# Tokens of a vision tower: one product of 128 rows per tile, coarse levels folded through the fusing matrix, table gathers issued without holds

## What is computed

```python
def _level(x, idx, W, b, p, gp):
    Bsz, C, H, _ = x.shape
    h = H // p
    t = x.reshape(Bsz, C, h, p, h, p).transpose(0, 2, 4, 3, 5, 1).reshape(Bsz, h * h, p * p * C)
    t = t[:, idx]
    t = t.reshape(Bsz, h * h // gp, gp * p * p * C)
    return t @ W.T + b
...
outs = [_level(x, idx, W, b, p, GP) for idx, W, b, p in Ws]
n_tokens = outs[0].shape[1]
outs = [outs[0]] + [_interp_linear(o, n_tokens) for o in outs[1:]]
y = jnp.concatenate(outs, axis=-1)
return y @ Wf.T + bf
```

## Time and profile before

| | |
|---|---|
| median of 3 runs | 1001.75 us (1001.4 to 1006.43) |
| profiled execution, first to last instruction | 1014.8 us |
| profiled execution, own time | not listed apart from its span |
| busy: TensorE, VectorE, ScalarE, GpSimd | 743.6, 697.2, 672.0, 345.9 us |
| mean granted TensorE clock | 0.796 |

### The profile page before, as it was taken

How to read it: one execution, slowest core, us unless ns; L and a number is a source line. 1 busy time by engine, 2 the same in 40 slices (tenths; PEclk the granted TensorE clock), 3 DMA queues, 4 the chain that set the end, 5 groups by cost and what they waited for, 6 DMA issues and landing times. The chain is left out here.

```text
span 1014.8 us, 19178 instructions
## 1 busy us (share of the span) xinstructions
PE 743.6 (73%) x7062; PEld 537.8 (53%) x7063; DVE 697.2 (69%) x1403; ACT 672.0 (66%) x1229; POOL 345.9 (34%) x260
## 2 busy tenths in 40 slices
PE   2987373344299547999997488867775898999985
PEld 1464141122277324589996444324444467899974
DVE  4159998999599888745443475986998875444542
ACT  1267956999799657755554369578983661676663
POOL 6620460000000000357776424580001202477763
PEclk9979555555599768999999879555556798999999
DMA  5224485000121318623333456380003942233332
GB/s 168 71 90 130 138 234 169 1 23 1 47 75 69 122 45 289 200 54 59 57 56 47 90 233 254 117 297 35 2 2 105 344 169 71 37 54 58 59 45 32
DMA packets 61883, 105.26 MB, mean 104 GB/s; under 512 B 9678, under 2 KB 43618, under 8 KB 61554
## 3 DMA queue, kind: packets, MB, share of 16 engines
q1 hardware_dynamic: 45426, 87.77, 25.6%
q0 software_dynamic: 16384, 16.53, 10.4%
HBM read 76.39 MB, written 27.87 MB: 103 GB/s over the span
## 5 line engine op out<-in xcount | busy, mean ns | idle before, releaser
L2301 DVE COPY m_xgT<-m_px 128x768 f16<-128x768 f16 (+1 forms) x46 | 22.9, 497 | 123.5 <-PE m_px L2146 123.5
L2268 ACT ACTIVATE m_pu<-m_pu,m_b,m_unit 128x256 f32<-128x256 f32 (+1 forms) x138 | 63.5, 509 | 60.9 <-PE m_pu L2178 58.4
L2309 DVE SCALAR_TENSOR_TENSOR m_hT<-m_pu,m_unit,m_hT 128x512 f16<-128x512 f32 (+1 forms) x138 | 86.4, 663 | 17.4 <-ACT m_hT L2261 17.2
L1084 ACT ACTIVATE a_ex<-m_pieces,a_nb 128x256 bf16<-128x256 f16 x192 | 94.6, 560 | 5.4 <-DVE a_nb L1110 5.4
L922 PE MATMUL a_pp<-a_room 16*128 16x256 bf16 x240 | 56.1, 412 | 39.8 <-DVE m_pieces L1098 31.9
L2272 ACT ACTIVATE m_pu<-m_pu,m_unit 128x512 f32<-128x512 f32 (+1 forms) x69 | 41.1, 597 | 62.7 <-PE m_pu L2178 61.7
L2261 ACT ACTIVATE m_hT<-m_pu,m_unit 128x512 f16<-128x512 f32 (+1 forms) x138 | 81.6, 636 | 0.0
L2112 POOL DMA_INDIRECT m_xg<-xn_d,m_token x70 | 70.0, 1000 | 32.1 <-issue 20.6
L2120 POOL DMA_INDIRECT out_h<-m_yo,m_token x39 | 62.1, 1593 | 40.6 <-DVE m_yo L2319 28.8
L2120 POOL DMA_INDIRECT h_d<-m_yo,m_token x39 | 62.1, 1592 | 37.3 <-DVE m_yo L2319 18.0
L2178 PE MATMUL m_pu<-m_xgT,m_w 128*128 128x256 f16 (+1 forms) x690 | 70.4, 261 | 1.3 <-DVE m_xgT L2301 1.3
(11 more groups left out here) (488 smaller groups left out, 1914.2 us busy)
## 6 DMA issues: line engine op xcount, KB each, us to landing
m_pieces<-in_m_w SPq DMA_DIRECT2D x11, 768.0 KB, 5.1
a_early_w<-in_m_w SPq DMA_DIRECT2D x10, 768.0 KB
hv_raw<-in_m_w SPq DMA_DIRECT2D x8, 768.0 KB, 6.2
w1h_d<-hv_parts SPq DMA_DIRECT2D x8, 768.0 KB, 4.1
m_w<-w1h_d SPq DMA_DIRECT2D x8, 768.0 KB, 9.0
m_pieces<-in_m_w SPq DMA_DIRECT2D x8, 576.0 KB, 5.3
a_room<-in_m_w SPq DMA_DIRECT2D x8, 576.0 KB, 3.6
hv_raw<-in_m_w SPq DMA_DIRECT2D x8, 576.0 KB, 5.9
```

What stands on the lines that cost most here:

```text
L1084: last = act.activation(ex[:, n % 2, r], v16t[:, n, r, :], ACT.Exp, bias=nbt[:, n, r:r + 1], scale=scale, accum_out=sumst[:, n, r:r + 1])
L2268: act.activation(pu[:, u, n, q * w:(q + 1) * w], pu[:, u, n, q * w:(q + 1) * w], ACT.Relu, bias=b1[:, bass.ds(e * FC + 2 * n + q, 1)], sca ...
L2309: last = v.scalar_tensor_tensor(hT[:, u, 1, third], pu[:, u, n, 0:2 * w], unit[:, 1:2], hT[:, u, 0, third], ALU.mult, ALU.subtract)
```

## The change

Each token tile becomes one product of 128 rows: its left operand `lt` holds, for one image, 64 rows of interpolation for the middle level and 64 rows of turned pixels (48) with interpolation for the coarsest level (16); its right operand `zz` holds the middle level's tokens after the fusing matrix, with all biases, and 64 rows with the folded fine matrix and the coarsest level's tokens after it. For odd and even images the two blocks of rows change places. W1 is folded through the fusing matrix ahead of the data (`w1f`), so the middle level needs one multiplication; all biases go through one product into `zb`, which VectorE adds. `seg` holds W0 and the coarsest level's tokens, and eight products by `wfe` turn it into the 64 rows of `zz`. The interpolation for the coarsest level is copied beside the pixels in `r0` and is turned with them, so one transpose serves two images; that for the middle level comes by four broadcasting DMAs. Base products, their evacuations and VectorE's additions go; ScalarE writes the fused tile to `h`. `HOLDS` is empty.

```diff
-        consts = ((c.ident[:], "ident"), (w1[:], "W1"), (w2[:], "W2"), (wf[:], "Wf"), (bl[:], "bl"), (w0[:], "W0"),
-                  (up[:], "up"), (bias[Z - 1:Z, :], "bf"), (c.identb[:], "identb"), (c.ident16[:], "ident16"))
+        consts = ((w1[:], "W1"), (wfm[:], "Wfm"), (c.ident[:], "ident"), (bl[:], "bl"), (wfe[:], "Wfe"), (w0[:], "W0"),
+                  (w2[:], "W2"), (up2[:], "up2"), (c.identb[:], "identb"), (c.ident16[:], "ident16"))
-        BANK = (2, 3, 0, 1)
+        BANK = (1, 2, 3, 0)
...
+                for half in range(2):
+                    for rows, first in ((slice(EMB, P), 0), (slice(0, EMB), 1)):
+                        sp.dma_start(lt[rows, half, first:B:2, :], a["up1"][:, half:half + 1, :]
+                                     .to_broadcast([EMB, B // 2, P])).then_inc(raised, 16)
                 proj.load(sp)
...
-                HOLDS = {6: (turned, 4), 10: (summed, 2), 20: (mixed, 4), 24: (turned, 6), 26: (fused, 4)}
+                HOLDS = {}
...
+                def turn_pixels(half, bank):
                     pe.wait_ge(ordered, 3 + half)
+                    for m in range(4):
+                        last = nc.tensor.transpose(bank[:, m * P:(m + 1) * P],
+                                                   r0[:, half, 2 * m:2 * m + 2, :].rearrange("p b f -> p (b f)"),
+                                                   c.ident[:])
+                    last.then_inc(turned, 1)
 
                 def fuse(half, m, bank):
                     for j in range(2):
+                        b = 2 * m + j
+                        last = nc.tensor.matmul(bank[:, j * D:(j + 1) * D], lt[:, half, b, :], zz[:, b, :],
                                                 start=True, stop=True)
...
+                for m in range(4):
+                    if m % 2 == 0:
+                        pe.wait_ge(kept, m // 2 + 1)
+                    for k in range(2):
+                        last = nc.tensor.matmul(po[:, m // 2, (m % 2) * D:(m % 2 + 1) * D],
+                                                f1[:, k, 2 * m * 64:(2 * m + 2) * 64], w1f[:, k, :],
+                                                start=(k == 0), stop=(k == 1))
...
+                pe.wait_ge(planted, 2)
+                for n in range(2):
+                    for k in range(4):
+                        r0_, j = EMB * (k % 2), k // 2
+                        last = nc.tensor.matmul(pt[r0_:r0_ + EMB, n, j * D:(j + 1) * D], seg[:, 4 * n + k, :], wfe[:],
+                                                start=True, stop=True)
+                    last.then_inc(mixed, 1)
...
+                for n in range(3):
                     weigher.total(act, n)
...
+                pixels(0, pt[:, 2])
                 for m in range(4):
+                    keep(0, m, po[:, m])
+                weigher.total(act, 3)
                 root(0)
...
                 take(0, 0, EACH)
-                pixels(1)
+                pixels(1, pt[:, 0])
+                for m in range(4):
+                    keep(1, m, pt[:, BANK[m]])
                 for n in range(4, 6):
                     weigher.total(act, n)
                 take(1, 0, 3)
```

More of the change, by code:

```diff
@@ L338, in embed @@
     nc = c.nc
-    Z = 97
     XS = 4096.0
@@ L586, in _ @@
[L586 to L590 removed]
+                nc.tensor.transpose(po[0:2, 3, 2 * P:3 * P], top[:, 0:2], c.ident[:]).then_inc(crossed, 1)
+                pe.wait_ge(planted, 2)
[3 more added lines that the diff above has]
+                        last = nc.tensor.matmul(pt[r0_:r0_ + EMB, n, j * D:(j + 1) * D], seg[:, 4 * n + k, :], wfe[:],
+                                                start=True, stop=True)
+                    last.then_inc(mixed, 1)
@@ new lines, in _ @@
+                pe.wait_ge(widened, 1)
+                nc.tensor.transpose(po[:, 3, 3 * P:3 * P + 2], wide[:], c.ident[0:2, 0:2]).then_inc(crossed, 1)
+                turn_pixels(0, pt[:, 2])
+                pe.wait_ge(raised, 64)
+                pe.wait_ge(kept, 5)
+                for m in range(4):
+                    pe.wait_ge(shifted, m // 2 + 1)
+                    pe.wait_ge(zkept, m // 2 + 1)
+                    if m == 3:
+                        pe.wait_ge(bkept, 1)
+                        pe.wait_ge(proj.weighed, 1)
@@ L591, in _ @@
                     fuse(0, m, po[:, m])
-                for n in range(4, 8):
-                    base(n)
                 for g in range(4):
@@ L639, in take, with pixels @@
                                .then_inc(taken, 1)
-                def pixels(half):
-                    for m in range(2):
-                        act.wait_ge(turned, 5 + 2 * half + m)
-                        act.activation(f0[:, half, 4 * m:4 * m + 4, :],
-                                       pt[0:48, m, :].rearrange("p (b t) -> p b t", b=4), ACT.Copy).then_inc(kept, 1)
+                def pixels(half, bank):
+                    act.wait_ge(turned, 5 + half)
+                    for first in range(2):
+                        rows = slice(first * EMB, (first + 1) * EMB)
+                        last = act.activation(lt[rows, half, first:B:2, :],
+                                              bank[rows, :].rearrange("p (b t) -> p b t", b=4), ACT.Copy)
+                    last.then_inc(kept, 1)
                 act.wait_ge(zeroed, 1)
@@ L662, in keep_base @@
-                def keep_base(n):
-                    half, m = n // 4, n % 4
-                    act.wait_ge(based, n + 1)
-                    act.activation(tiles[:, half, 2 * m:2 * m + 2, :], pair(po[:, m]), ACT.Copy).then_inc(hkept, 1)
-                for n in range(4):
-                    keep_base(n)
-                pixels(0)
-                for n in range(2, 4):
-                    weigher.total(act, n)
-                for n in range(4, 8):
-                    keep_base(n)
+                for n in range(2):
+                    act.wait_ge(mixed, n + 1)
+                    for first in range(2):
+                        rows = slice(first * EMB, (first + 1) * EMB)
+                        last = act.activation(zz[rows, 4 * n + first:4 * n + 4:2, :], pair(pt[rows, n]), ACT.Copy)
+                    last.then_inc(zkept, 1)
@@ L674, in _, with keep @@
+                def keep(half, m, bank):
+                    act.wait_ge(fused, 4 * half + m + 1)
+                    act.activation(tiles[:, half, 2 * m:2 * m + 2, :], pair(bank), ACT.Copy).then_inc(hkept, 1)
+                pixels(0, pt[:, 2])
+                for m in range(4):
+                    keep(0, m, po[:, m])
+                weigher.total(act, 3)
                 root(0)
```

202 lines of the change are left out of this document (86 added, 116 removed).

## The result

The changed kernel takes 1004.72 us in the median of 17 runs (1001.05 to 1008.06), against 1001.53 (997.62 to 1006.77) for 17 runs of the kernel before beside them. The ratio is 1.0035, 95% interval 1.002 to 1.005: **slightly slower**, by 2 to 5 us. The forecast was 994.6 and its range ended at 1001.5; the ratio lies within the 0.5% that the prediction called the same, on its slower side. The profiled execution of the changed kernel took 1005.97 us, close to the median.

The account below looks back on a forecast made before the run. The token stage was taken as bound by the chain to the first layernorm reciprocal, then ScalarE's second root and VectorE. Terms 1.0 - 11.0 + 0.7 + 2.1 = -7.2 us, off the median 1001.75: 994.6 us; range 989.5 to 1001.5.

Parts of the forecast that it names:

- The base (the sum's last sentence): End of the sum: the -7.2 us, priced on the profiled 1014.8 us execution, applied to the median 1001.75, giving 994.6.
- The 3.38 us hand-over: First half: idle TensorE-to-ScalarE hand-over at 51.04, ended by nothing the profile names; its 3.38 us counted in the -11.0.
- The late root: First half: ScalarE's root, at 62.95 behind four evacuations of second-half base products; about 3 us counted in the -11.0.
- What follows ... I take it to shift as one piece: Everything behind the token stage does the same work, so the time shifts by the shift of the stage's end.
- Part 1: Loads: four interpolation broadcasts, 0.52 MB, share the DMA engines with the coarse gathers; +1.0 us, bounds 0 and +3.
- Part 2: Coarse levels on TensorE: products of 4.9, 3.67 and 6.3 us, to 38.9; VectorE then scales weights and orders pixels, to 42.3.
- Part 3: Fine gathers without holds: the sixteenth lands at 37.5, before VectorE asks at 41.9; removed holds alone are worth nothing.
- Part 4: First fuse: 4.9 us of products, last at 49.5; first reciprocal at 52.2 against 63.19, -11.0 us.
- Part 5: First reciprocal to second pixels: 10.2 us as before, plus 0.7 for TensorE's lower clock level.
- Part 6: Second half: four added ScalarE evacuations delay the root; reciprocal at 83.3 against 81.15, +2.1 us.
- that rival: Unheld gathers stretched by VectorE: the last lands at 61 to 63 instead of 57.5, +3 us (997.5); chance 0.12.
- The clock did not fall for the whole stage: Rival: TensorE falls to its lower clock level for the whole token stage, 1004 us, slower; chance 0.10.

Follow-up runs that it names:

- the second, third and fourth profile: The kernel before, unedited, profiled again, one run each: 997.63, 1000.46 and 1005.98 us.
- the fifth: The kernel before, unedited, profiled again, one run: 998.21 us.
- the kernel with 99 products: The kernel before plus 99 tiny products of zeros on TensorE where it waits for its constants: 1003.62 us, ratio 1.0016 (0.9985 to 1.0048).
- that with 41: The changed kernel plus 41 tiny products on TensorE where it waits for its constants: 1002.6 us, ratio 1.001 (0.9984 to 1.0036).
- the earlier root: The changed kernel with ScalarE's second root ahead of the third take and two weight pieces behind it: 1003.69 us, ratio 1.0028 (1.0004 to 1.0052).
- the changed kernel with 29 products: The changed kernel plus 29 tiny products on TensorE where it waits for its constants: 1001.2 us, ratio 1.001 (0.9978 to 1.0042).

## Why the prediction was wrong, point by point

**The base (the sum's last sentence) is the step that failed.** "I apply the difference to the median": the terms priced an execution whose stage ended at 105.66, and the median execution's ends near 96.2 (the middle of five). Two of the terms in the -11.0 were of that execution. The 3.38 us hand-over is in none of the later profiles of this kernel: none has an idle time ended by "remote" in the stage. The late root, 3.17 us of VectorE's waiting at 63.19, is 0.33 or 0.34 in the second, third and fourth profile and 1.50 in the fifth, where the second half's base products again ran at the lower level in part (4.55 us; 5.05 in the first profile, 3.02 in the other three) and ScalarE's evacuations of them held the root:

```profile
48.63 4.55 PE L582 MATMUL po<-m_pieces,up 97*128 97x192 f32 x16
...
52.05 0.28 DVE L730 TENSOR_SCALAR ln_rs<-ln_mv 128x8 f32<-128x8 f32 x1
...
53.60 0.20 ACT L613 ACTIVATE ln_sd<-ln_rs 128x8 f32<-128x8 f32 x1
53.84 0.20 DVE L732 RECIPROCAL ln_rs<-ln_sd 128x8 f32<-128x8 f32 x1 [1.50 <-ACT ln_sd L613]
```

So the wait that the sum counted as saved was there, but its usual size was a tenth of what the profile showed. What ended the hand-over stays open. Against the five profiles' middle, the first half gains 52.6 - 48.8 = 3.8 us and the whole stage 96.2 - 93.5 = 2.8 us, where the sum had 11.0 and 7.2; with ends from 91.30 to 105.66, that middle is known to a few us only. The sign that I passed over was in the rows: the earlier trace rows print a clock of 1.00 for 13 to 20 us, but nothing was recorded before 48.3, and one and the same L526 took 3.97 and 2.83 us.

**"What follows ... I take it to shift as one piece" failed too**, and the prediction had named this as what would break it. Between profiles taken together, the block of the scores became 3.5 us longer (153.2 and 156.7; 154.0 to 154.1 and 157.6), since the change shortened TensorE's code by 81 instructions (11760 to 11679) and moved an instruction fetch from 42.0 to 51.3 us behind the stage's end. The timelines of the kernel with 99 products and of that with 41 show this in both directions.

**Part 1** (+1.0): the coarse gathers were ordered at 18.90 after, against 18.38 in the first profile: +0.5, inside its bounds. In the other profiles it was 18.16 to 19.27 before and 18.46 and 18.87 after, so the term can't be told from nothing, and no run shows the half rate of its upper bound. **Part 2**: 4.92 for the middle level's eight products was right (4.9). The eight by `seg` took 1.52 us instead of 6.3. The clock is part of it: 0.785 was a product at the lower level, 0.43 to 0.47 at the higher one in the second profile of before. That the new ones need only 0.19 each no run here explains. W2 took 1.96, not 3.67; at the higher level it took 1.91 in the kernel before too. TensorE's coarse work was over at 32.7 instead of 38.9 and a transpose. **Part 3**: the claim that the gathers land at 37.5, "before the 41.9 at which VectorE asks", was 1 us early on the landing (38.5) and wrong about who waits: VectorE asked at 35.35 and waited 3.20 us. This is the cover that I had missed: with TensorE done by 33, GpSimd's queue of gathers bounds the half, and at 58.59 the second (2.96). **Part 4**: the fuse took 4.74 (4.9 forecast), reciprocal 48.80 (52.2 forecast). **Part 5**: 59.81 - 48.80 = 11.0 us from the reciprocal to the second pixels, against 10.9 forecast. **Part 6** had the mechanism right: 9.15 us from the second pixels to the reciprocal, about 9.8 forecast, and 7.7 in the kernel before's first two profiles, so +1.4 instead of +2.1; the earlier root took back 2.55 of the 9.15.

**The rivals.** No hand-over came late in the changed kernel. The gathers were hardly stretched (median 0.944, the longest 1.48), though VectorE's wait for the second half's gathers, the sign named for that rival, did appear: the last of them was issued at 56.3, 1.1 us behind 31 steps of 1.25 from 16.47, and not the 3.5 to 5.5 of that rival. VectorE waited because it asked earlier than forecast. The clock did not fall for the whole stage: 1.00 in most of 55 to 90 us. The slower result came from none of the rivals.

The balance: by the middles of the table the stage has -2.8 and the scores +2.7 (154.0 and 156.7), and the two added, execution by execution, end at 250.3 us before (244.5 to 258.6) and at 250.1 after (250.0 to 251.5). The gain of the stage is eaten up in the scores, and the medians say +3.2 (2 to 5). **What stays open** is that rest, about 3 us. Behind the scores the profiles of either kernel spread by 8 us and more. One long stretch, the experts of the first layer (some 118 us), took 117.8 to 120.1 us in nine profiles with TensorE's code at the length of before, and 119.3 to 121.7 in five with the changed length, 1.6 us more in the mean; in the three with 29 or 99 products it took 117.8 to 118.4. In the unedited ones alone it is 117.8 to 118.8 and 119.3 to 120.8. That would fit another fetch at a bad place, and the 1001.2 us of the changed kernel with 29 products; but the kernel before without holds, with TensorE's code unchanged, took 120.1, and I have not shown it.

## What to carry to other kernels

Before pricing terms from one profile, look whether it is a typical execution: compare its span with the runs, and compare one operation's duration at two places; here the first half of one and the same kernel's stage took 48 to 63 us, and most of the difference was the clock under TensorE's small products. Ask of each gain which queue stands right behind it, here the gathers at 1.25 us each: work taken from the engine that was last is worth only the distance to the next one. And when a time moves in a block that no edit touched, look at its last transfers part by part, and at the instruction fetches, before blaming memory or luck.

## What was not expected of the hardware

One 16 KB instruction fetch, 1.07 us long, in the midst of a burst of weight loads made one of 16 parts of three successive loads late by 1.4, 1.9 and 3.2 us, more than its own length; 1.0 us long and ahead of the burst it cost nothing. Why the delay grows beyond the fetch, no run here shows. In all 17 profiles the fetch stood at 41.9 to 43.0 or at 50.8 to 52.4 us behind the stage's end, never between, with TensorE's code 0 or 1 instruction longer than before in the first case, and 23, 58 and 81 shorter in the second (the 58 are 198 longer less one fetch of 256). How the length picks the moment, no run here shows.
